# Gradient scores of a 256-channel patch selection: edges of patches apart, inner differences single

## The reference, cut to what matters

```python
g = x.reshape(4, 32, 8, 256, 256)
v = ((g - mean(g)) / sqrt(var(g) + 1e-5)).reshape(x.shape)
ex = conv(v, [-1, 0, 1], along columns)      # zero padding
ey = conv(v, [-1, 0, 1], along rows)         # zero padding
s = 0.5 * (abs(ex) + abs(ey)) + 0.5 * abs(v)
sp = s.reshape(4, 256, 8, 32, 8, 32).mean(axis=(3, 5)).reshape(4, 256, 64)
ranks = argsort(argsort(-sp, axis=1), axis=1)
mask = (ranks < 128)                         # per channel and patch
out = x + v * mask (spread over each patch)
```

## Time and profile before

| | us |
|---|---|
| runs | 2267.05, 2267.48, 2268.71 |
| median | 2267.48 |
| the profiled execution | 2268.49 |
| its span | 2266.8 |
| mean granted clock of TensorE, of full speed | 0.841 |
| busy PE / DVE / ACT / POOL | 1629.9 / 1810.7 / 1652.5 / 1259.3 |
| DMA moved | 776.88 MB |

### The profile page before, as it was taken

How to read it: one execution, slowest core, us unless ns; L and a number is a source line. 1 busy time by engine, 2 the same in 40 slices (tenths; PEclk the granted TensorE clock), 3 DMA queues, 4 the chain that set the end, 5 groups by cost and what they waited for, 6 DMA issues and landing times.

```text
span 2266.8 us, 21900 instructions
## 1 busy us (share of the span) xinstructions
PE 1629.9 (72%) x5960; PEld 952.7 (42%) x5960; DVE 1810.7 (80%) x2282; ACT 1652.5 (73%) x2581; POOL 1259.3 (56%) x925
## 2 busy tenths in 40 slices
PE   6888888868888888868888888878888888700000
PEld 3555555544544444434544444544445444400000
DVE  7999999989888888879898888889888988782232
ACT  5778777769888889879888889788988888800000
POOL 5667666747666666637666666647666666400000
PEclk9999999979988888979888889978898888855555
DMA  7633335328999999796999999898999999499999
GB/s 297 259 149 148 148 148 222 149 84 347 418 412 412 413 408 409 322 407 277 407 418 415 408 401 410 339 398 347 410 411 408 415 416 380 195 419 428 432 433 389
DMA packets 41261, 776.88 MB, mean 343 GB/s; under 512 B 4576, under 2 KB 4576, under 8 KB 4576
## 3 DMA queue, kind: packets, MB, share of 16 engines
q1 hardware_dynamic: 41184, 775.96, 82.5%
HBM read 507.51 MB, written 268.44 MB: 342 GB/s over the span
## 4 chain that ended last, share of the span: by engine, by line
ACT 31%; PE 21%; issue 15%; DVE 13%; DMA 9%; DVEq 4%; POOL 4%; ACTq 1%; SPq 0%; POOLq 0%
ACT again L528 16%; ACT thrown L575 10%; DMA out_dram<-ring 7%; PE vertical L449 5%; PE vertical L450 4%; PE vertical L453 4%; DVE stats L613 4%; DVEq L604 4%; DMA ring<-in_x_dram 3%; POOL across L272 3%; ACT vertical L562 3%; PE vertical L455 2%; PE vertical L431 2%; DVE sums L644 2%; DVE records L649 2%
## 5 line engine op out<-in xcount | busy, mean ns | idle before, releaser
L272 POOL TENSOR_TENSOR across<-ring 128x1920 f32<-128x1920 f32 x240 | 813.0, 3388 | 0.0
L613 DVE BATCH_NORM_STATS2 stats<-ring 128x6 f32<-128x512 f32 x960 | 589.6, 680 | 8.8 <-DMA ring<-in_x_dram 5.7
L575 ACT ACTIVATE thrown<-ring,record 128x1024 bf16<-128x1024 f32 x480 | 549.0, 1144 | 38.1 <-DVE record L620 33.4
L263 POOL TENSOR_TENSOR across<-ring 128x32 f32<-128x32 f32 x240 | 187.4, 781 | 650.2 <-DVE record L620 452.7
L449 PE MATMUL vertical<-ring,plus 128*128 128x512 f32 x600 | 383.4, 725 | 187.6 <-ACT vertical L562 187.6
L644 DVE TENSOR_REDUCE sums<-across 128x2 f32<-128x2048 f32 x212 | 481.9, 2273 | 9.3 <-POOL across L272 9.3
L562 ACT ACTIVATE vertical<-vertical 128x1024 f32<-128x1024 f32 x320 | 322.5, 1008 | 204.6 <-PE vertical L431 204.6
L528 ACT ACTIVATE again<-again,coef 128x1024 f32<-128x1024 f32 x360 | 416.9, 1236 | 0.0
L453 PE MATMUL vertical<-ring,plus 128*128 128x512 f32 x600 | 366.2, 695 | 0.0
L450 PE MATMUL vertical<-ring,minus 128*128 128x480 f32 x600 | 339.4, 652 | 0.0
L635 DVE TENSOR_TENSOR down_ps<-ring 128x960 f32<-128x960 f32 x120 | 309.9, 2583 | 0.2 <-issue 0.2
(11 more groups left out here) (117 smaller groups left out, 1947.6 us busy)
## 6 DMA issues: line engine op xcount, KB each, us to landing
ring<-in_x_dram SPq DMA_DIRECT2D x66, 4096.0 KB, 19.1
...
```

Of the source, the lines that this page charges most:

```text
L272: nc.gpsimd.tensor_tensor(d[:, :, :, 1:PATCH - 1], xs[:, w:w + 2, :, 2:PATCH], xs[:, w:w + 2, :, 0:PATCH - 2], ALU.subtract)\
L575: nc.scalar.activation(thrown[:], patch(buffer, w), ACT.Abs, bias=record[r][:, 2:3], accum_out=sums[r][:, 2, w:w + 1]).then_inc(centred, 1)
L613: nc.vector.bn_stats(stats[:, k, :], buffer[:, k * BN:(k + 1) * BN])
```

## The change

Every patch's edge rows and columns are now made apart from its inside. TensorE makes the two edge rows of all 8 patches in one PSUM bank, `border_bank` (one matmul 512 wide, four 256 wide), and of patches 0 to 4 the inner 30 rows in four matmuls (512, 512, 448 and 448 wide), without borders. GpSimd makes the inner columns patch by patch (30 x 32, eight instructions, four buffers), the edge columns of all patches in four small instructions, and the inner rows of patches 6 and 7 (contiguous, 960 elements, one buffer, step `p` of ScalarE). VectorE keeps the inner rows of patch 5 (step `d`), sums the rows and the columns at the edges (512 elements each), and sums half of the inner columns in the first image and all in the others. `sums` has five kinds. The mean of the next tile is made before TensorE's last patch (in the first image before the last two); TensorE and GpSimd start a tile when it is loaded instead of at `minus_mean`; VectorE starts a tile with statistics; the first three elements of a record are kept by a reduction instead of a multiplication. `wait_done_with` counts single patches. In the last tile of an image the variance is now taken up after `minus_mean`, and GpSimd makes one inner difference after its power. `PE_PATCHES` stays 5.

```diff
+INSIDE = (PATCH - 2) * PATCH
 PE_PATCHES = 5
-DVE_PATCHES = COLS - PE_PATCHES
-PAIRS = COLS // 2
+DOWN_DVE, DOWN_POOL = 5, (6, 7)
+SLOTS_ACROSS = 4
+ACROSS = (0, 5, 2, 1, 3, 4, 7, 6)
...
-ORDER_FIRST = "a a d0 v0 a a h0 v1 a a v2 d2 h1 a v3 a v4".split()
-ORDER = "a a d0 v0 a d1 a v1 o a v2 d2 a v3 o a a v4".split()
-ORDER_AFTER_RANKING = "a a d0 v0 h0 a a v1 h1 a a v2 h2 a a v3 h3 k k d1 d2 v4 o".split()
+ORDER_FIRST = "h0 a0 v0 a1 h2 v1 a2 h1 p6 d h3 a3 v2 a4 a5 a6 a7 v3 p7 v4".split()
+ORDER = "o a0 a1 v0 a2 a3 v1 o a4 v2 a5 p6 d a6 a7 v3 p7 v4".split()
+ORDER_AFTER_RANKING = "a0 h0 v0 h5 a1 h2 v1 h1 a2 h3 a3 h4 v2 a4 a5 h7 a6 v3 a7 k k d p6 p7 h6 v4".split()
...
-        across = [sb(f"across{b}", [PARTS, 2, PATCH, PATCH]) for b in range(2)]
-        scratch = sb("scratch", [PARTS, 3 * AREA // 2])
-        down_sb = scratch[:, 0:AREA].rearrange("p (r c) -> p r c", r=PATCH)
+        across = [sb(f"across{b}", [PARTS, PATCH, PATCH - 2]) for b in range(SLOTS_ACROSS)]
+        edges = sb("edges", [PARTS, COLS, 2, PATCH])
+        scratch = sb("scratch", [PARTS, CHANNELS + AREA])
...
-        vertical = [pb(f"vertical{b}", [PARTS, PATCH, PATCH]) for b in range(2)]
-        down_ps = pb("down_ps", [PARTS, PATCH, PATCH])
-        down = [down_ps[:], down_sb]
-        small_bank = pb("small_bank", [PARTS, 512])
+        vertical = [pb(f"vertical{b}", [PARTS, AREA]) for b in range(2)]
+        down_dve = pb("down_dve", [PARTS, AREA])[:, 0:INSIDE]
+        down_pool = scratch[:, 0:INSIDE]
+        border_bank = pb("border_bank", [PARTS, 2 * WIDTH])
+        mean_bank = rank_bank[:, 511:512]
...
+            def inner_across(tile, buffer, w):
+                n = ACROSS.index(w)
+                slot = n % SLOTS_ACROSS
+                xs = by_patch(buffer)
+                pool.wait_ge(across_free[slot], len(ACROSS) // SLOTS_ACROSS * tile + n // SLOTS_ACROSS + CREDIT_ACROSS)
+                nc.gpsimd.tensor_tensor(across[slot][:], xs[:, w, :, 2:], xs[:, w, :, 0:PATCH - 2], ALU.subtract)\
+                    .then_inc(across_ready, 1)
+            def inner_down(tile, buffer, w):
+                n = DOWN_POOL.index(w)
+                v = patch(buffer, w)
+                pool.wait_ge(down_pool_free, len(DOWN_POOL) * tile + n + CREDIT_DOWN)
+                nc.gpsimd.tensor_tensor(down_pool, v[:, 2 * PATCH:], v[:, 0:INSIDE], ALU.subtract)\
+                    .then_inc(down_pool_ready, 1)
+            def columns_at_edge(tile, buffer, r):
                 xs = by_patch(buffer)
                 nm = record[r][:, 2:3]
+                pool.wait_ge(edges_free, tile + CREDIT_EDGES)
+                nc.gpsimd.tensor_tensor(edges[:, 1:, 0, :], xs[:, 1:, :, 1], xs[:, 0:COLS - 1, :, PATCH - 1],
+                                        ALU.subtract)
+                nc.gpsimd.tensor_tensor(edges[:, 0:COLS - 1, 1, :], xs[:, 1:, :, 0], xs[:, 0:COLS - 1, :, PATCH - 2],
+                                        ALU.subtract)
                 pool.wait_ge(minus_mean_ready, tile + 1)
-                for k in range(PAIRS):
...
+                nc.gpsimd.tensor_tensor(edges[:, 0, 0, :], xs[:, 0, :, 1], nm.broadcast_to([PARTS, PATCH]), ALU.add)
+                nc.gpsimd.tensor_tensor(edges[:, COLS - 1, 1, :], xs[:, COLS - 1, :, PATCH - 2],
+                                        nm.broadcast_to([PARTS, PATCH]), ALU.add).then_inc(edges_ready, 1)
+            def differences(tile, buffer, r, loaded, count):
+                pool.wait_ge(loaded, 16 * count)
+                for w in (0, 5, 2, 1):
+                    inner_across(tile, buffer, w)
+                inner_down(tile, buffer, 6)
+                inner_across(tile, buffer, 3)
+                inner_across(tile, buffer, 4)
+                columns_at_edge(tile, buffer, r)
+                inner_across(tile, buffer, 7)
+                inner_down(tile, buffer, 7)
+            def differences_during_ranking(tile, image):
+                pool.wait_ge(ring_loaded[0], 16 * LOOPED * image)
+                for w in (0, 5, 2, 1, 3, 4):
+                    inner_across(tile, ring[0], w)
+                columns_at_edge(tile, ring[0], 0)
+                inner_across(tile, ring[0], 7)
+                pool.wait_ge(mask_ready, image)
+                inner_down(tile, ring[0], 6)
+                inner_down(tile, ring[0], 7)
+                inner_across(tile, ring[0], 6)
...
+            def rows_at_edge(tile, buffer, r):
                 xs = by_patch(buffer)
+                beyond = record[r][:, 2:3].broadcast_to([PARTS, WIDTH])
+                top, bottom = border_bank[:, 0:WIDTH], border_bank[:, WIDTH:]
+                pe.wait_ge(border_free, tile + CREDIT_BORDER)
+                nc.tensor.matmul(border_bank[:], plus[:],
+                                 xs.rearrange("p w r c -> p r w c")[:, 1:PATCH - 1:PATCH - 3],
+                                 start=True, stop=False)
+                nc.tensor.matmul(top, from_above[:], xs[:, :, PATCH - 1, :], start=False, stop=False)
+                nc.tensor.matmul(bottom, from_below[:], xs[:, :, 0, :], start=False, stop=False)
                 pe.wait_ge(minus_mean_ready, tile + 1)
+                nc.tensor.matmul(top, at_top[:], beyond, start=False, stop=False)
+                nc.tensor.matmul(bottom, at_bottom[:], beyond, start=False, stop=True).then_inc(border_ready, 1)
...
+            def inner_down(tile, buffer, patches):
                 for w in patches:
+                    v, xs = vertical[w % 2], patch(buffer, w)
                     pe.wait_ge(vertical_free, PE_PATCHES * tile + max(w - 1, 0) + CREDIT_VERTICAL)
+                    for first, end in ((0, AREA // 2), (AREA // 2, INSIDE)):
+                        nc.tensor.matmul(v[:, first:end], plus[:], xs[:, first + 2 * PATCH:end + 2 * PATCH],
+                                         start=True, stop=False)
+                        done = nc.tensor.matmul(v[:, first:end], minus[:], xs[:, first:end], start=False, stop=True)
+                    done.then_inc(vertical_ready, 1)
+            def tile_work(tile, buffer, r, loaded, count, after, mean_before):
+                pe.wait_ge(loaded, 16 * count)
+                inner_down(tile, buffer, (0, 1))
+                rows_at_edge(tile, buffer, r)
+                inner_down(tile, buffer, range(2, mean_before))
                 mean(tile + 1, after)
+                inner_down(tile, buffer, range(mean_before, PE_PATCHES))
...
+            def inner_down(tile, buffer):
+                v = patch(buffer, DOWN_DVE)
+                dve.wait_ge(down_dve_free, tile + CREDIT_DOWN)
+                nc.vector.tensor_tensor(down_dve, v[:, 2 * PATCH:], v[:, 0:INSIDE], ALU.subtract)\
+                    .then_inc(down_dve_ready, 1)
+            def across_sum(tile, r, w):
+                n = ACROSS.index(w)
+                slot = n % SLOTS_ACROSS
+                dve.wait_ge(across_ready, COLS * tile + n + 1)
+                nc.vector.tensor_reduce(sums[r][:, INNER_ACROSS, w:w + 1], across[slot][:], AX.XY, ALU.add,
+                                        apply_absolute_value=True).then_inc(across_free[slot], 1)
+            def columns_at_edge(tile, r):
+                dve.wait_ge(edges_ready, tile + 1)
+                nc.vector.tensor_reduce(sums[r][:, COLUMNS_AT_EDGE, :], edges[:], AX.XY, ALU.add,
+                                        apply_absolute_value=True).then_inc(edges_free, 1)
+            def rows_at_edge(tile, r):
+                dve.wait_ge(border_ready, tile + 1)
+                nc.vector.tensor_reduce(sums[r][:, ROWS_AT_EDGE, :],
+                                        border_bank[:].rearrange("p (a w c) -> p w a c", a=2, w=COLS), AX.XY, ALU.add,
+                                        apply_absolute_value=True).then_inc(border_free, 1)
+            def keep_statistics(r, t):
+                nc.vector.tensor_reduce(records[:, bass.ds(t, 1), 0:3].rearrange("p a k -> p (a k)"),
+                                        record[r][:].unsqueeze(2), AX.X, ALU.add)
             def keep_record(tile, r, t):
                 wait_analysed(dve, tile + 1)
-                nc.vector.tensor_scalar(records[:, bass.ds(t, 1), 0:3].rearrange("p a k -> p (a k)"),
-                                        record[r][:], 1.0, None, ALU.mult)
+                keep_statistics(r, t)
...
+            def first_image_step(g, u, before, after, count):
+                tile = RING * g + u
+                buffer = places[u]
...
+                next_statistics(0)
+                across_sum(tile, u, 5)
+                next_statistics(1)
+                inner_down(tile, buffer)
+                next_statistics(2)
+                next_statistics(3)
+                if before is not None:
+                    keep_record(tile - 1, before, tile - 1)
+                across_sum(tile, u, 4)
+                columns_at_edge(tile, u)
+                rows_at_edge(tile, u)
+                minus_mean(tile + 1, after)
```

(48 more changed lines are left out.)

267 lines of the change are left out of this document (106 added, 161 removed).

## The result

The changed kernel takes 2167.54 us (median of 4 runs, 2166.37 to 2169.20), the kernel before beside it 2267.81: ratio 0.9558, 95% interval [0.9545, 0.957]. The forecast was 2167.

The account below looks back on a forecast made before the run. VectorE was taken to bound the first image, a ScalarE-TensorE loop the streamed tiles, DMA the tail. First image -37, ranking +3, middle images -47, last image -20: -101 from 2268.5, giving 2167 us (range 2128 to 2214).

Parts of the forecast that it names:

- The ring through ScalarE's `v0`: Streamed tile before: ScalarE idles 3.96 us ahead of `v0`, as TensorE begins that patch only after ScalarE's last sum.
- Of the 3.96 at most 0.4 is left: Streamed tile: with `o a a` (6.8 us) ahead of `v0`, ScalarE's wait of 3.96 us falls to at most 0.4.
- The 483 us of an image: Middle images: DMA becomes the bound, 197.1 MB at 422 GB/s is 467 us, plus 16 idle; bounds 472 and 494.
- Rival 1: Streamed tiles: DMA stays at 414 GB/s, middle images take 494 us, total 2200; chance 0.22.
- 15 tiles of 27.35 us, bound by VectorE: First image before: VectorE, busy 375.4 of 410.2 us, sets the tile of 27.35 us.
- what closes the tile *after* the change: First image: TensorE's `v0` starts behind the previous `v4`, half clock in about half the patches; tile 24.9, gain 37 us.
- rival 3: A new wait: `v0` always at half clock in the first image (26.8), or ScalarE waiting for GpSimd's buffer; 2196; chance 0.07.
- Net +3 (bounds -1 and +7): Ranking: about 7 us added to its path, two standstills save some 1.7 each, so 3 us longer.
- The two standstills of 4.24 and 4.23: Ranking: two instructions behind a GpSimd instruction of 3.4 us then stand at most 1.7, saving some 1.7 each.
- GpSimd no longer waits for `minus_mean` at a tile's start: Tile's start: GpSimd begins without `minus_mean`; its work is 19.4 us a tile plus a wait of 1.1 for VectorE.
- Between the others it partly lies beside DMA: Rankings after image 1: the added time is partly covered by DMA, while in image 1 it counts in full.
- Rivals 4 and 5: All stages slower: TensorE's clock stays down, near 2890, chance 0.03; or GpSimd's short instructions stay dear, near 2640, chance 0.02.

Follow-up runs that it names:

- b_order: Kernel before with only the first `o` of ORDER moved from behind `v3` to the head of the tile: 2191.0 us, ratio 0.9659.
- a_oback: Changed kernel with the first `o` of ORDER moved from the head of the tile back to behind `a7 v3`: 2230.89 us.
- a_halfstore: Changed kernel storing only the first half of each half-tile that was read again in the streamed images, the rest left out: 2069.37 us.
- b_record: Kernel before with only the copy of three numbers in keep_record made by a reduction: 2268.07 us, ratio 0.9999.
- b_swap: Kernel before with the next tile's `minus_mean` placed ahead of VectorE's last pair sum instead of behind it: 2235.66 us, ratio 0.9858.
- a_hold: Changed kernel with GpSimd not beginning the next image's first tile until the last image's patch scores are there: 2146.6 us, ratio 0.9463.
- a_latemean: Changed kernel with TensorE's mean of the next tile put back behind all five patches: 2162.44 us.
- b_cheap: Kernel before with two reorderings only, first `o` at the head of the tile and `minus_mean` ahead of the last pair sum: 2148.83 us, ratio 0.9478.

## Why the prediction was right, and where its steps were not

**Streamed tiles and middle images: right.** The ring through ScalarE's `v0` was there and closed the tile: b_order removes it, a_oback restores it, 3.9 and 3.7 us a tile. "Of the 3.96 at most 0.4 is left" holds, and the tile becomes DMA's (a_halfstore). The 483 us of an image were 467 of transfer at 422 GB/s and 16 of idleness. Measured, the mean is again 483 (486.2 and 479.7). Counted from the shares, as the forecast was, DMA idles 0.04 x 483 = 19 us and moves 197.1 MB in the other 464 at 425 GB/s: both terms within 3 us. The choice of 422 as the middle of 414 and 430 was a guess, though, that came out. The rate is not one number either: nine late tiles ran at 431, the four ahead of them at 422 (978.6 to 1084.5, share 1.01). Rival 1, 414 GB/s for good, is refuted by 431.

The Trainium skill, "DMA: Bandwidth & Descriptors", section "Where 436 GB/s comes from", gives 358 as the binding side and 435 as the ceiling. The trace comes within 1% of the second for hundreds of microseconds, with one core at work; the first does not bind here.

**First image: the sum held, its reason did not.** The step "15 tiles of 27.35 us, bound by VectorE" failed. b_record took 2.3 us of VectorE's work out of every tile for nothing, b_swap took none out and won 2.4 us a tile. The bound was the ring of GpSimd's pairs, the last sum and `minus_mean`. The step on what closes the tile *after* the change was sound: `v4`, then `v0` at a low clock. Forecast 24.9 with half of the patches at half clock; measured 25.1 (25.0 in the 13 even tiles), with every such patch at half clock at its start, for 4.96 to 6.33 us, 5.4 in the mean. Between 3.5 and 7.0 that is near the middle, but by another route: that the number fits is luck in this step. The tile was also reached from the wrong side, since the ring that the change opened was not the one named. The 15 tiles gained 33 us instead of 37. The patch itself at full clock was forecast at 3.5 and takes 3.22, since its 512 columns pass in 0.86 where the row used had 0.94. Another 7.2 us came ahead of the second tile, which the forecast had not set apart; it makes up for most of the 4 us missing here and the 5 lost in the ranking, so the sum came out.

The Trainium skill, "TensorE: Matmul & The Clock Gate", section "HAM oscillation — how this bites in real kernels", warned that a burst behind a wait starts at half clock each time. So the trace shows it in the first image, tile by tile (0.91 granted there). The 26.8 us that rival 3 drew from it did not come, because the full clock was back within the patch, in two of three tiles behind two or three of its four pairs of matmuls.

**Ranking: the term that was mis-sized.** "Net +3 (bounds -1 and +7)", measured +8.1, just outside its bounds. By ranking the interval grew by 8.2, 7.7 and 9.1 us. The 7 us put ahead of the scale chain were about right (6.2, 7.1, 7.1). The two standstills of 4.24 and 4.23 are gone, 3.1 us each in the second and third ranking instead of the 1.7 forecast, but 0.6 and 1.9 of it went into a wait for TensorE. In the first ranking there was less to gain: its standstills were 3.48 (L731) and 3.26, and all that lies behind the scores' chain got only 1.2 us shorter. What was missed: the chain used to run while GpSimd was at its short edge columns or waited for `minus_mean`; now GpSimd's next tile runs beside it. From its first instruction to the end of the scores it took 1.5 us in the second ranking and takes 6.4; 4.6 and 7.8 in the first; in a_hold, with GpSimd idle beside it, it takes 1.35. The prediction listed it as a gain that "GpSimd no longer waits for `minus_mean` at a tile's start" and did not ask who had been running undisturbed in that wait. "Between the others it partly lies beside DMA" did not show either: in a_hold each ranking's microseconds count in nearly full.

**GpSimd: too low, without effect.** Forecast 19.4 us a tile, measured 21.5: 1.8 for a single difference (1.7), 2.22 for one down (1.7), 1.0 and 1.58 for the edge columns (0.8). It waits 372.9 us for ScalarE in the run, so nothing came of it. VectorE (22 forecast, 21.9), ScalarE (26.2, 26.4) and the free mean (a_latemean) were right.

**Rivals 4 and 5** did not come: the granted clock in streamed tiles is 0.88, and no single difference is over 2.3 us in the mean.

**What the change is worth by parts**: 63 us the place of one `o` (77 where it is moved alone); 37 the rest, most of it the first image's ring less the ranking's loss. The swap in b_swap brings the second tile of image 2 to 470.0 us, the whole change to 471.5. b_cheap gains in the same stages by two moved steps and loses less in the ranking (13.1 to 13.3 us).
